# A feed-forward's turning and way out moved between engines and steps, idle products in an attention, and meetings that pass over next weights

## The reference

```python
for i in range(DEPTH):
    x = x + self_attention(layer_norm(x, ln1_g[i], ln1_b[i]), Wq[i], Wk[i], Wv[i], Wo[i], bo[i])
    h = layer_norm(x, ln2_g[i], ln2_b[i])
    x = x + (jax.nn.gelu(h @ W1[i] + b1[i], approximate=False) @ W2[i] + b2[i])
```

```python
qkv = shift_token(x) @ wqkv
q, k = rotary_xpos(l2norm(q) * qs, l2norm(k) * ksc)
#   q * cos * scale + rotate_half(q) * sin * scale    (k with 1 / scale)
x = x + local_attention(q, k, v) @ wo
h = norm(shift_token(x)) @ w1 + b1
a, g = jnp.split(h, 2, axis=-1)
x = x + (a * gelu(g)) @ w2 + b2
```

## Time and profile before

| | us |
|---|---|
| median of 3 runs | 5559.17 |
| lowest, highest | 5528.2, 5561.08 |
| the profiled execution | 5561.03 |
| its span | 5559.7 |
| busy PE, DVE, ACT, POOL | 3955.6, 2958.9, 1909.0, 883.2 |
| mean granted clock of PE, share of full speed | 0.774 |

### The profile page before, as it was taken

One profiled execution on the slowest core, in us unless ns is written; L12 is line 12 of the kernel. 1 busy time (PEld: TensorE's weight loads), 2 busy tenths in 40 slices (PEclk: granted clock), 3 DMA queues, 4 the chain that ended last, 5 costly groups with the idle time before them and its releaser, 6 DMA issues.

```text
span 5559.7 us, 94810 instructions
## 1 busy us (share of the span) xinstructions
PE 3955.6 (71%) x39676; PEld 3058.5 (55%) x39676; DVE 2958.9 (53%) x7957; ACT 1909.0 (34%) x4228; POOL 883.2 (16%) x664
## 2 busy tenths in 40 slices
PE   5786958467878778772757768586777777776388
PEld 4674847355555555552646556474444555545277
DVE  4445464325555555547255565656666666665233
ACT  2233232123333333330232332324455555552122
POOL 0000000231111101112600000002222211120544
PEclk6555565588989999885856666668899999997699
DMA  9200000240000000001200000000000000000255
GB/s 270 55 2 1 2 1 2 77 145 1 1 1 1 1 1 1 1 7 34 44 26 1 1 1 2 1 2 2 1 1 1 1 1 1 1 1 17 83 163 139
DMA packets 140860, 152.33 MB, mean 27 GB/s; under 512 B 7808, under 2 KB 128002, under 8 KB 139792
## 3 DMA queue, kind: packets, MB, share of 16 engines
q1 hardware_dynamic: 119024, 128.21, 7.8%
q0 software_dynamic: 21408, 18.05, 1.9%
HBM read 87.38 MB, written 59.76 MB: 26 GB/s over the span
## 4 chain that ended last, share of the span: by engine, by line
PE 48%; DVE 30%; ACT 13%; issue 4%; POOL 3%; DMA 2%; another core or an unknown queue 1%; SPq 0%; DVEq 0%; POOLq 0%; ACTq 0%
ACT work L3251 4%; PE banks_lane L801 4%; PE banks_lane L422 3%; PE banks_lane L3689 2%; PE banks_lane L1885 2%; DVE work L2038 2%; PE banks_lane L809 2%; PE banks_lane L3137 2%; PE banks_lane L935 2%; PE banks_lane L3172 1%; PE banks_lane L3117 1%; DVE work L2806 1%; PE banks_lane L3159 1%; DVE weights L3261 1%; ACT work L1983 1%
## 5 line engine op out<-in xcount | busy, mean ns | idle before, releaser
L422 PE MATMUL banks_lane<-constants,work 128*128 128x128 f32 x968 | 195.0, 347 | 455.0 <-DVE work L408 210.5
L422 PEld LDWEIGHTS banks_lane<-constants,work 128*128 128x128 f32 x968 | 146.5, 179 | 522.2 <-DVE work L408 197.3
L402 POOL TENSOR_TENSOR weights<-weights,constants 128x4 f32<-128x4 f32 x76 | 78.5, 1033 | 1928.1 <-DVE weights L397 1928.1
L422 PE MATMUL banks_lane<-constants,weights 128*128 128x128 f32 x596 | 124.0, 344 | 355.1 <-DVE weights L408 93.2
L422 PEld LDWEIGHTS banks_lane<-constants,weights 128*128 128x128 f32 x596 | 87.6, 177 | 386.5 <-issue 169.1
L3251 ACT ACTIVATE work<-banks_lane,weights 128x192 f32<-128x192 f32 (+1 forms) x512 | 249.1, 506 | 127.3 <-DVE weights L3345 127.3
L402 POOL TENSOR_TENSOR work<-work,constants 128x4 f32<-128x4 f32 x76 | 77.3, 1018 | 1146.0 <-DVE work L397 1146.0
L3352 POOL TENSOR_TENSOR weights<-weights,constants 128x16 f32<-128x16 f32 x64 | 185.4, 2896 | 211.6 <-DVE weights L3263 211.6
L2038 DVE TENSOR_REDUCE work<-banks_lane 128x2 f32<-128x512 f32 x256 | 158.7, 683 | 77.7 <-PE banks_lane L1899 77.5
L3341 DVE TENSOR_REDUCE weights<-banks_lane 128x2 f32<-128x384 f32 (+1 forms) x256 | 122.4, 520 | 141.4 <-PE banks_lane L3159 141.4
L3172 PE MATMUL banks_lane<-constants,work 128*128 128x128 f32 x896 | 133.2, 294 | 79.3 <-DVE work L3333 41.5
(11 more groups left out here) (780 smaller groups left out, 10801.8 us busy)
## 6 DMA issues: line engine op xcount, KB each, us to landing
work<-experts_dram_l_ffn SPq DMA_DIRECT2D x39, 964.0 KB
room_l_ffn<-work SPq DMA_DIRECT2D x30, 1188.0 KB, 14.4
work<-experts_dram_l_ffn SPq DMA_DIRECT2D x23, 512.0 KB
weights<-weights_dram SPq DMA_DIRECT2D x1, 4833.5 KB, 14.4
work<-room_l_ffn SPq DMA_DIRECT2D x36, 132.0 KB
weights<-weights_dram SPq DMA_DIRECT2D x1, 4112.0 KB, 12.8
weights<-bands_dram SPq DMA_DIRECT2D x1, 4096.0 KB, 13.2
weights<-room_l_ffn SPq DMA_DIRECT2D x26, 132.0 KB
```

Source lines behind the costliest of these rows:

```text
L402: pool.tensor_tensor(n.rstd, n.rstd, c("neghalf", cols=(0, n.rstd.shape[1])), ALU.pow).then_inc(*u.pool.step(name))
L422: done = pe.transpose(bank[0:rows, t * P:(t + 1) * P], block, c("ident"))
```

## The change

- *Meetings.* `Run.meet` passes over the two semaphores of the weight transfers. The waits for a stage's own weights (`weights_landed`) stay.
- *Idle products.* `keep_busy` issues products of the bfloat16 identity with the 512-wide mask `later` whose result nobody reads. In the second attention each unit issues two behind a wait for `kT`, before the first scores; each unit of the last lane issues 14 behind the `inverses` transposes, into bank 2.
- *Third feed-forward, sine part.* For queries DVE no longer adds cos and sin parts; PE multiplies each block of both with the identity and accumulates them in the bank, two products instead of one transpose. Keys stay as they were. ACT's squares of the next tile, which write the memory of `m.sin`, wait for that turning.
- *Third feed-forward, way out.* The way-out products of tile t - 1 (`out_pe`) are issued in the first group's step of tile t, behind the wait for ACT's copy of the turned weights and before the values, into bank 3. DVE's addition follows behind the weights' multiplication of that step. Turning in the second group's step waits for it (its bank 3); the turning of the first group's waits only for the `oT` copy. The last tile's way out stays where it was. The phases `out0` to `out3` become one, `out`, so lanes alternate without them.

```diff
+WEIGHTS = [("DMA", f"weights{n}") for n in range(2)]
...
     def meet(self, engine):
-        for s in self.steps.values():
-            if s.count:
+        for key, s in self.steps.items():
+            if s.count and key not in WEIGHTS:
                 engine.wait_ge(s.sem, s.count)
...
+def keep_busy(pe, masks, bank, n):
+    for _ in range(n):
+        pe.matmul(bank[:, :], masks("ident"), masks("later"))
...
+L1_ATTN_NORM_FILL, L1_ATTN_SCORE_FILL = 14, 2
...
             if r == 0:
+                pe.wait_ge(*u.act.at("kT"))
+                keep_busy(pe, self.masks, b[1], L1_ATTN_SCORE_FILL)
                 pe.wait_ge(*u.act.at("v1"))
...
         made.then_inc(*u.pe.step("inverses"))
+        if u.lane == LANES - 1:
+            keep_busy(pe, self.masks, b[2], L1_ATTN_NORM_FILL)
         yield "inverses"
...
                 for j in range(L2_FFN_PAIRS):
-                    made = pe.transpose(bank[:, cols_of(j)], m.cos[:, n, cols_of(j)], c("ident"))
+                    if n:
+                        made = pe.transpose(bank[:, cols_of(j)], m.cos[:, 1, cols_of(j)], c("ident"))
+                    else:
+                        pe.matmul(bank[:, cols_of(j)], m.cos[:, 0, cols_of(j)], c("ident"), start=True, stop=False)
+                        made = pe.matmul(bank[:, cols_of(j)], m.sin[:, 0, cols_of(j)], c("ident"), start=False, stop=True)
                 made.then_inc(*u.pe.step(f"flipped{t}_{n}"))
...
             yield f"turn{t}_{group}"
+            pe.wait_ge(*u.act.at(f"turned{t}_{group}"))
+            if group == 0 and t > 0:
+                self.out_pe(pe, u, t - 1, b[3])
             self.values_pe(pe, u, t, group, n)
             yield f"values{t}_{group}"
-            if group == 1:
-                pe.wait_ge(*u.act.at(f"oT{t}_1"))
-                for j in range(L2_FFN_PAIRS):
-                    made = pe.matmul(b[2][:, 0:P], m.oT[:, cols_of(j)], self.w(u, f"o{j}"), start=j == 0,
-                                     stop=j == L2_FFN_PAIRS - 1)
-                made.then_inc(*u.pe.step(f"projected{t}"))
-                yield f"out{t}"
+        self.out_pe(pe, u, TILES - 1, b[2])
+        yield "out"
...
+    def out_pe(self, pe, u, t, bank):
+        m = self.lanes[u.lane]
+        pe.wait_ge(*u.act.at(f"oT{t}_1"))
+        for j in range(L2_FFN_PAIRS):
+            made = pe.matmul(bank[:, 0:P], m.oT[:, cols_of(j)], self.w(u, f"o{j}"), start=j == 0, stop=j == L2_FFN_PAIRS - 1)
+        made.then_inc(*u.pe.step(f"projected{t}"))
...
             pe.wait_ge(*u.act.at(f"oT{pt}_{pg}"))
-            if pg == 1:
-                pe.wait_ge(*u.dve.at(f"attended{pt}"))
         for side in ((0, 1) if t else (1,)):
+            if side and group == 1 and t > 0:
+                pe.wait_ge(*u.dve.at(f"attended{t - 1}"))
...
                     act.wait_ge(*u.dve.at(f"roped{t - 1}_1"))
+                    act.wait_ge(*u.pe.at(f"flipped{t - 1}_0"))
...
+                if n == 0:
+                    u.dve.mark(f"roped{t}_0")
+                    continue
                 dve.wait_ge(*u.dve.last())
-                dve.tensor_tensor(m.cos[:, n, :], m.cos[:, n, :], m.sin[:, n, :], ALU.add).then_inc(*u.dve.step(f"roped{t}_{n}"))
+                dve.tensor_tensor(m.cos[:, 1, :], m.cos[:, 1, :], m.sin[:, 1, :], ALU.add).then_inc(*u.dve.step(f"roped{t}_1"))
...
                 self.weights_dve(dve, u, *L2_FFN_STEPS[n + 1], n + 1)
+            if group == 0 and t > 0:
+                dve.wait_ge(*u.pe.at(f"projected{t - 1}"))
+                dve.tensor_tensor(y[:, t - 1, :], y[:, t - 1, :], b[3][:, 0:P], ALU.add).then_inc(*u.dve.step(f"attended{t - 1}"))
             yield f"values{t}_{group}"
```

More of the change, by code:

```diff
@@ L3178, in values_pe @@
         m, sides = self.lanes[u.lane], (0, 1) if t else (1,)
-        pe.wait_ge(*u.act.at(f"turned{t}_{group}"))
         if t:
@@ L3271, in dve @@
                     dve.tensor_tensor(turned[:, :, lo:lo + half], src[:, :, frm:frm + half], every_head64(sin[:, lo:lo + half]),
-                                      ALU.mult).then_inc(*u.dve.step())
+                                      ALU.mult).then_inc(*u.dve.step(f"turned{t}_{side}"))
+                if n == 0:
+                    u.dve.mark(f"roped{t}_0")
+                    continue
                 dve.wait_ge(*u.dve.last())
-                dve.tensor_tensor(m.cos[:, n, :], m.cos[:, n, :], m.sin[:, n, :], ALU.add).then_inc(*u.dve.step(f"roped{t}_{n}"))
+                dve.tensor_tensor(m.cos[:, 1, :], m.cos[:, 1, :], m.sin[:, 1, :], ALU.add).then_inc(*u.dve.step(f"roped{t}_1"))
             dve.wait_ge(*u.pool.at(f"roots{t}"))
@@ L3298, in dve @@
                 self.weights_dve(dve, u, *L2_FFN_STEPS[n + 1], n + 1)
+            if group == 0 and t > 0:
+                dve.wait_ge(*u.pe.at(f"projected{t - 1}"))
+                dve.tensor_tensor(y[:, t - 1, :], y[:, t - 1, :], b[3][:, 0:P], ALU.add).then_inc(*u.dve.step(f"attended{t - 1}"))
             yield f"values{t}_{group}"
-            if group == 1:
-                dve.wait_ge(*u.pe.at(f"projected{t}"))
-                dve.tensor_tensor(y[:, t, :], y[:, t, :], b[2][:, 0:P], ALU.add).then_inc(*u.dve.step(f"attended{t}"))
-                yield f"out{t}"
+        dve.wait_ge(*u.pe.at(f"projected{TILES - 1}"))
+        dve.tensor_tensor(y[:, TILES - 1, :], y[:, TILES - 1, :], b[2][:, 0:P], ALU.add).then_inc(
+            *u.dve.step(f"attended{TILES - 1}"))
+        yield "out"
         yield "shift again"
```

## The result

| us | before | after |
|---|---|---|
| median of 6 runs each | 5556.19 | 5490.06 |
| lowest, highest | 5528.2, 5561.08 | 5482.48, 5501.7 |
| profiled execution, its span | 5561.03, 5559.7 | 5487.05, 5485.7 |
| mean granted clock | 0.774 | 0.783 |

The ratio is 0.9895, with a 95% interval of 0.9878 to 0.9911. On a second chip, beside runs of before there, it was 0.9878 (0.9860 to 0.9897). The forecast was 5480 us with a range of 5440 to 5520, and faster by over 1%. The median lies 10 us above the forecast and in the range. The gain is 58 us by the ratio (49 to 68) where 79 were forecast, and the interval of the ratio still reaches to 0.9%.

The account below looks back on a forecast made before the run. The prediction took the kernel to be bound by dependences, no engine being full. Terms of -9, -42 and -28 gave -79 against the profiled 5561.0, 5482, and 5480 us for the median, range 5440 to 5520.

Parts of the forecast that it names:

- Meetings: Two stalls of 7.4 and 2.0 us, waiting for the next stage's weights, vanish: 9.4 us gained.
- idle products: Second attention's norm gaps: filling keeps the clock full behind them, 2.0 us in each of 16, taken as -28 us.
- way out, with the give-back: Third feed-forward: 57 us leave 24 places between tiles; 5 us are given back for overflow at low clock.
- sine part: Third feed-forward projections: PE takes over as bound from DVE, costing +1.3 us per pair of batches, +10 us in all.
- almost nothing to spare: Third feed-forward attention step: PE's 8.24 us of work fits into the step's 8.39 us.
- the rival of the overflow: Way-out products overflow their step in the third feed-forward: 0.95 us per step uncovered, 5498 us; chance 0.09.
- the 5 given back: Third feed-forward: 0.6 us per pair returned because PE's work overflows the first steps at low clock.
- the ten slow places: Ten of 24 way-out places in the third feed-forward, at low clock, counted as 30.5 us saved together.
- Forecast pace: Third feed-forward projections: one lane and tile goes from 5.44 to 5.86 us.
- the tail: End of the third feed-forward's projections: two DVE additions fewer before the last key turning, -1.2 us per pair.
- The second rival, more clock: Low clock vanishes in more places of the third feed-forward and second attention: 5450 us; chance 0.17.
- turning products cost twice: Third feed-forward turning products take 0.22 us a record instead of 0.11: 5580 us, slower than before; chance 0.07.

Follow-up runs that it names:

- meetings: Kernel before with only the meetings changed (no wait for the next stage's weights): ratio 0.9985 (0.9969 to 1.0001) to before.
- way_out_later: Kernel before with only the third feed-forward's way-out products issued a tile later: ratio 0.9930 (0.9906 to 0.9954) to before.
- after_again: The kernel after, unchanged, run once more on a second chip: ratio 0.9878 (0.9860 to 0.9897) to before, median 5474.0 us.
- third_idle_no_sine: Kernel after without the queries' sine products on PE, with four more groups of idle products in the third feed-forward: ratio 0.9812 to before, median 5424.4 us.
- Sine_part: Kernel before with only the queries' sine part added by PE's turning products: ratio 1.0014 (1.0003 to 1.0025) to before.
- no_sine: Kernel after without the queries' sine products, DVE adding again: ratio 0.9872 (0.9856 to 0.9889) to before, median 5475.4 us.
- third_idle: Kernel after with three more groups of idle products in the third feed-forward: ratio 0.9834 (0.9818 to 0.9851) to before, median 5435.8 us.

## Why the prediction was nearly right, term by term

The mechanisms were right. By the timed runs three of the four sizes were too, and the way out was put 13 us too high. The sine part's +10 meets the timed +8 partly by luck: the reason given for it, the pace, costs 4 to 5 us. The range, 80 us wide, was as wide as the forecast gain, so that the median lies in it is no close test. The terms are the closer one.

| us | forecast | timed alone | stage in the traces |
|---|---|---|---|
| meetings | -9.4 | -8 (-17 to +1) | -6 in the third attention (-2 to -4 on the chip of meetings), the 2 of the second not to be told apart |
| idle products | -28 | -27 (-37 to -17) | -31 with those 2; some 7 of it chance |
| way out, with the give-back | -52 | -39 (-52 to -26) | -35 |
| sine part | +10 | +8 (+2 to +14) | 0 alone, -12 within the whole (0 timed) |
| sum | -79 | -66; the whole, timed: -58 and -68 | -74 for the whole |

**Way out: right mechanism, 13 us too much.** The turning of the next weights follows in all 24 places straight behind the oT copy, and the step absorbs nearly all of the products, as forecast. Two sizes were off. PE's work in a step was put at 8.24 us; it is 8.60, because ways out and values alternate and each group then begins 1.02 to 1.09 us before the next, where 1.0 and 0.93 were assumed. So "almost nothing to spare" was less than nothing, the rival of the overflow is true by 0.21 us a step, and a tile saves 1.62 instead of 1.89: 24 by 0.27, 6.5 us, against the 5 given back. The step that failed is the pricing of the ten slow places at what they took (30.5 for ten). 10 by 1.62 is 16; the 14 us above it were a debt of the clock, time lost because an idle stretch ahead had brought the clock down, and not of the way out. Half clock in the eight pairs' attention is 103 us in before and 102 in way_out_later: it moved to the places that are left. 24 by 1.62 is 39, what was timed; the attention alone is 38 shorter, of which the rest of the pairs gives 3 back.

**Sine part: pace right, sum too high.** Forecast pace 5.86, seen 5.80: from the turning's start to the next projection it is 3.11 us (4659.50 to 4662.61) where 3.17 were summed. PE bounds the phase instead of DVE: it idles only before a projection, and DVE is busy for 41.2 us of 52.8, where it was for 45.6 of 53.4. The pace adds 6 by 0.36, 2.2 us per pair; the tail gives back 1.6, not 1.2 (last projection to last keys' turning 7.97 us instead of 9.55): +0.6, where full clock shows +0.5 and the forecast had +1.3. The second rival, more clock, is what the traces show on top: with the sine part the projections of the last seven pairs are at half clock for 0 to 1.5 us, without it for 6.8 to 8.6. The forecast had seen that the filled idle might do this and gave it up to 2 us per pair. That is not seen: with the sine part alone, what the projections gain the attention gives back.

The rival "turning products cost twice" is excluded. Sixteen records take 1.78 us and four transposes 0.44 (4684.47 to 4684.91 in after): a block's pair of float32 products is 0.45, one product 0.22, a transpose 0.11. The Trainium skill's factor ("TensorE: Matmul & The Clock Gate", Terms: transpose mode 4 times faster for float32) is 2 in these rows. The measurement decides.

**Idle products: right in place, the size partly from elsewhere.** Gap 5.0, fill 3.0, idle left 2.0, and 2.0 us saved per gap that is followed by full clock: nine to eleven of the 16, not all. With what the other gaps save, 22 to 24 of the 28 us are found at the place; the rest of the timed 27 (17 to 37) can't be told from other stretches of the stage. That a fill longer than its gap costs time, as the forecast assumed, was seen with 28 products. The clock still falls now and then behind the 2.0 us that are left, in after_again (1.98 is the gap ahead of the second lane's norm):

```profile
1683.72 0.66 PE L425 MATMUL banks_lane<-constants,work 128*128 128x128 f32 x4 [2.03 <-DVE work L411]
...
1684.44 0.54 PE L1888 MATMUL banks_lane<-weights,work 128*128 128x128 f32 x2
1684.78 0.64 PE L1887 MATMUL banks_lane<-weights,work 128*128 128x128 f32 x2
...
1693.23 0.66 PE L425 MATMUL banks_lane<-constants,work 128*128 128x128 f32 x4 [1.98 <-DVE work L411]
```

**Meetings.** The wait of 7.4 us is gained in full at the first norm, is still there 51 us into the stage, and 2 to 6 us are left at the end of the stage. So no other producer was as late, and the rival is excluded. What takes the rest back later in the stage, no run shows.

**What stays open.** Sine_part was timed 8 us slower than before while its stage is level, and no_sine level with after_again while its stage is 12 us longer. Differences of this size between single executions cover both (the first attention was 979 to 986 us without any edit there, the third feed-forward of after 1220 to 1237), but no run separates them. Nor was it tried whether the sine products keep the clock up because they are longer than a transpose or because they are another kind of work. That nine idle products in the same gap keep it up in most pairs (third_idle_no_sine) speaks for the filled time.

## What to carry to other kernels

Price a slow stretch at its full-clock length first, and treat the excess as a debt of the idle stretch ahead of it. Here moving the slow work didn't pay that debt (way_out_later), and filling the idle stretches did (third_idle). When work is moved into a step with almost no margin, count each group from its start to the next group's start in the new neighbourhood, since the tails that the old neighbours covered may not be covered. Idle products should end before the gap does; their worth is judged over the whole stage, because half clock that is driven out of one gap can come back at another, as it did with 28 products.

## What the runs showed of the hardware

- The same instructions were at half clock for 249 us in one execution of the second attention and for 296 and 297 in others, and took 1264 or 1284 us; the third feed-forward of after varied between 1220 and 1237. A difference of one trace in such a stage is good to some 10 to 20 us only.
- How often the granted clock fell, from full, in or up to 1.5 us behind an idle time of PE, in the traces of before and after together. Third feed-forward: 6 of 300 idle times of 0.6 to 1.3 us, 23 of 69 of 1.3 to 1.9, and 34 of 36 of 1.9 to 3.2. Second attention: 54 of 216 of 0.6 to 1.3 us, none of 27 of 1.3 to 1.9, 24 of 37 of 1.9 to 2.3, and all 23 longer ones. So the length of the one idle time before it doesn't settle a fall.
- More work on PE made a phase shorter: 43.1 us of work in 52.8 against 36.0 in 53.4. It is the clock, since at full clock the phase is 52.3 us without the added work and 52.8 with it. Filling three idle stretches per pair took half clock in a stage from 173 to 57 us and 25 us off its time.
